# A decoder layer on one core: the output projection in float32r parts, its lower part made on VectorE

## What is computed

```
q = _l2norm((x @ Wq)...); k = _l2norm((x @ Wk)...); v = x @ Wv
alpha = sigmoid(x @ Wg)
S = a_t[..., None] * S + k_t[..., None] * v_t[:, :, None, :]
o_t = einsum('bhkv,bhk->bhv', S, q_t)
return o @ Wo                                   # 8 heads of 128
...
alpha = softmax(X_src @ (X_tgt @ W.T).T); return alpha @ X_tgt
...
h = gelu(x @ Wd[top 2 of 8] + bd) * top_w;  out = h @ Wu + top_w * bu
```

## Time and profile before

| | us |
|---|---|
| three runs | 504.81, 505.24, 506.90 |
| median | 505.24 |
| the profiled execution | 506.75 |
| its span (first to last instruction) | 504.9 |
| PE busy in the span | 469.6 |
| PEld / DVE / ACT / POOL busy | 387.0 / 364.5 / 337.8 / 107.7 |
| Wo matmuls L1232, busy | 60.7 |

### The profile page before, as it was taken

How to read it: one execution, slowest core, us unless ns; L and a number is a source line. 1 busy time by engine, 2 the same in 40 slices (tenths; PEclk the granted TensorE clock), 3 DMA queues, 4 the chain that set the end, 5 groups by cost and what they waited for, 6 DMA issues and landing times.

```text
span 504.9 us, 23866 instructions
## 1 busy us (share of the span) xinstructions
PE 469.6 (93%) x10212; PEld 387.0 (77%) x10212; DVE 364.5 (72%) x1058; ACT 337.8 (67%) x797; POOL 107.7 (21%) x102
## 2 busy tenths in 40 slices
PE   1799999999999999999999999999999999989556
PEld 1588788877888788778888788778888888768334
DVE  5777887655789698774779698774778688863671
ACT  4858777666777857788577867787578858665311
POOL 1022222111221121242121121242022021230130
PEclk9979999999999999999999999999999999998957
DMA  8900000001010010022101010022100010020121
GB/s 325 321 3 5 3 5 3 4 3 44 5 34 15 3 45 3 4 66 66 44 15 34 3 45 4 3 67 65 44 3 5 3 45 3 10 81 0 43 64 61
DMA packets 15256, 20.15 MB, mean 40 GB/s; under 512 B 1200, under 2 KB 12976, under 8 KB 15152
## 3 DMA queue, kind: packets, MB, share of 16 engines
q1 hardware_dynamic: 13872, 14.43, 8.8%
q0 software_dynamic: 1280, 4.20, 2.8%
HBM read 16.53 MB, written 2.10 MB: 37 GB/s over the span
## 4 chain that ended last, share of the span: by engine, by line
PE 49%; DVE 9%; ACT 5%; issue 4%; POOL 1%; DMA 1%; ACTq 0%; DVEq 0%; POOLq 0%
PE ring L1121 13%; PE acc L1232 7%; PE ring L1134 5%; PE lo_bank L1145 5%; PE ring L1213 4%; PE hi_bank L1204 2%; PE ring L1283 2%; PE ring L1220 2%; PE ring L1301 1%; PE ring L1267 1%; PE hi_bank L1176 1%; DVE states L690 1%; PE ring L1293 1%; DVE stats L660 1%; ACT probs L507 1%
## 5 line engine op out<-in xcount | busy, mean ns | idle before, releaser
L466 ACT COPY states<-states 128x512 f32<-128x512 f32 x128 | 80.9, 632 | 46.8 <-DVE states L690 31.2
L379 POOL TENSOR_TENSOR rnorm<-norm_sq,neg_half 128x4 f32<-128x4 f32 x32 | 44.8, 1400 | 267.9 <-DVE norm_sq L753 267.9
L690 DVE TENSOR_TENSOR states<-states,spans 128x512 f32<-128x512 f32 x96 | 66.4, 692 | 10.0 <-PE hi_bank L1176 2.5
L1145 PEld LDWEIGHTS lo_bank<-states 128*32 128x32 f32 x5120 | 51.1, 110 | 23.2 <-issue 19.3
L1232 PE MATMUL acc<-wo_sb,oT_sb 128*128 128x256 f32 x256 | 60.7, 380 | 0.7 <-ACT oT_sb L493 0.7
L1145 PE MATMUL lo_bank<-states 128*32 128x16 f32 (+1 forms) x5120 | 57.9, 188 | 0.0
L741 DVE COPY_PREDICATED blocks<-owned,lo_bank 128x64 f32<-128x64 uint32 (+1 forms) x160 | 41.0, 256 | 22.2 <-PE lo_bank L1145 17.6
L1134 PE MATMUL ring<-wv_sb,xnT 128*128 128x256 f32 x384 | 55.7, 295 | 1.3 <-DVE wv_sb L946 1.3
L1121 PE MATMUL ring<-xnT,wk_sb 128*128 128x512 f32 x192 | 53.7, 416 | 2.0 <-DVE xnT L809 1.6
L1121 PE MATMUL ring<-xnT,wq_sb 128*128 128x512 f32 x192 | 53.4, 413 | 0.0
L1121 PE MATMUL ring<-xnT,wg_sb 128*128 128x512 f32 x192 | 51.8, 406 | 0.4 <-DVE wg_sb L946 0.3
(11 more groups left out here) (157 smaller groups left out, 783.4 us busy)
## 6 DMA issues: line engine op xcount, KB each, us to landing
x_buf<-x_dram SPq DMA_DIRECT2D x4, 512.0 KB, 4.3
ctxT_sb<-ctxT_dram SPq DMA_DIRECT2D x8, 256.0 KB, 3.5
ctx_sb<-ctx_dram SPq DMA_DIRECT2D x4, 512.0 KB, 3.9
out_dram<-x_mid SPq DMA_DIRECT2D x6, 256.0 KB, 2.3
states<-wk_dram SPq DMA_DIRECT2D x1, 1024.0 KB, 5.6
states<-wg_dram SPq DMA_DIRECT2D x1, 1024.0 KB, 7.7
states<-wq_dram SPq DMA_DIRECT2D x1, 1024.0 KB, 9.8
v_sb<-wv_dram SPq DMA_DIRECT2D x1, 1024.0 KB, 11.8
```

The lines of the kernel that those rows point to most:

```text
L379: nc.gpsimd.tensor_tensor(rnorm[:, m % 4, GB:2 * GB], norm_sq[:, GB:2 * GB], neg_half[:, GB:2 * GB], ALU.pow).then_inc(rk_set, 1)
L466: nc.scalar.copy(halves(l, 2 ** (l - 1), False), halves(l - 1, 2 ** (l - 1), False)).then_inc(carry_set, 1)
L690: nc.vector.tensor_tensor(halves(l, w, True), halves(l - 1, w, True), by, ALU.mult).then_inc(decayed, 1)
L1145: last = mm(lo_bank[BLOCK * r:BLOCK * r + BLOCK, to:to + columns], view(states, left + start, [[1, BLOCK]]), view(states, right + start, q ...
```

## The change

- `wo_sb` gets two float32r parts. Wo is loaded by four DMAs (two heads each) into `x_mid` and `rowsT`, which are idle at the start; at the "end" of units 0, 2, 4 and 6 ACT copies the upper part of two heads (128x512) and DVE subtracts the lower (128x512).
- `oT_sb` is float32r with the places HI and LO instead of two alternating buffers. ACT's copy writes HI and now waits until Wo of the unit before has been read (`wo_read_by`); a new DVE instruction `oT_lower(n-2)` reads the same PSUM bank, subtracts HI and writes LO. It stands behind `q_decayed(n+1)` and ahead of tail "late". Wo and the ring's bank wait for it (`oT_lo`).
- Wo of a unit is 12 float32r matmuls of 128x256 instead of 4 float32 ones.
- In the fourth head (h = 3) the eight transposes of the next group's rows move from slot "A" (ahead of `attend`) to slot "B" (behind Wo); ACT's and DVE's reads of them move to the end of the unit.
- `ctx_sb` is now a view of `ctxT_sb`. The plain context is loaded when the transposed one has been used (behind the keys at h = 7), the next transposed one behind the cross attention. So three times the two loads only trade places; the last plain context moves from behind the cross attention of unit 28 to behind the keys of unit 31, and the first is no longer loaded at the start.

```
-        wo_sb = sb("wo_sb", [P, H, D])
+        wo_sb = sb("wo_sb", [P, 2, H, D], F32R)
...
-        ctx_sb = sb("ctx_sb", [P, GB, D])
         ctxT_sb = sb("ctxT_sb", [P, KC, GB, T])
+        ctx_sb = ctxT_sb[:].rearrange("p c b t -> p (c b t)").rearrange("p (b d) -> p b d", b=GB)
...
             if place == "A" and h == 3:
                 found = [("probsT", t, 0)] if t >= 0 else []
-                found += [("xT", i + 1, 0), ("xT", i + 1, 1)] if i + 1 < NG else []
+            if place == "B" and h == 3 and i + 1 < NG:
+                found = [("xT", i + 1, 0), ("xT", i + 1, 1)]
...
-                        "o": (o_set, n + 1), "oT": (oT_set, n + 1)}[kind]
+                        "o": (o_set, n + 1), "oT": (oT_lo, n + 1)}[kind]
...
             for i in range(1, NG):
                 sp.wait_ge(tail_mm, TAIL["keys", i - 1, 1])
-                load_ctxT(i)
+                load_ctx(i - 1)
...
                 sp.wait_ge(tail_mm, TAIL["cross", i - 1, 1])
-                load_ctx(i)
+                load_ctxT(i)
+            sp.wait_ge(tail_mm, TAIL["keys", NG - 1, 1])
+            load_ctx(NG - 1)
...
             def oT_out(n):
                 act.wait_ge(oT_mm, n + 1)
-                nc.scalar.copy(oT_sb[:, n % 2], ring_of(("oT", n))[:]).then_inc(oT_set, 1)
+                if n > 0:
+                    act.wait_ge(*wo_read_by(n - 1))
+                nc.scalar.copy(oT_sb[:, HI], ring_of(("oT", n))[:]).then_inc(oT_set, 1)
...
+            def split_wo(j):
+                act.wait_ge(wo_in, 16 * WO_PAIRS)
+                nc.scalar.copy(wo_sb[:, HI, 2 * j:2 * j + 2].rearrange("p h d -> p (h d)"), stage_o[j]).then_inc(wo_hi, 1)
...
+            def oT_lower(n):
+                dve.wait_ge(oT_set, n + 1)
+                nc.vector.tensor_tensor(oT_sb[:, LO], ring_of(("oT", n))[:], oT_sb[:, HI].bitcast(F32),
+                                        ALU.subtract).then_inc(oT_lo, 1)
...
+                if n >= 2:
+                    oT_lower(n - 2)
                 tail_part(n, "late")
...
             tail_part(U, "late")
+            oT_lower(U - 2)
             o_scaled(U - 1)
+            oT_lower(U - 1)
...
-                    last = mm(accs[z][:, D * m:D * m + D], oT_sb[:, n % 2, T * b:T * b + T], wo_sb[:, h],
-                              start=(h == 0 and m == 0), stop=(h == H - 1 and m == 1))
+                    for part, (a, w) in enumerate(PARTS):
+                        last = mm(accs[z][:, D * m:D * m + D], oT_sb[:, a, T * b:T * b + T], wo_sb[:, w, h],
+                                  start=(h == 0 and m == 0 and part == 0), stop=(h == H - 1 and m == 1 and part == 2))
```

More of the change, by code:

```diff
@@ L101, in decoder_kernel @@
         o_sb = sb("o_sb", [P, GB, P])
-        oT_sb = sb("oT_sb", [P, 2, N])
+        oT_sb = sb("oT_sb", [P, 2, N], F32R)
         x_mid = sb("x_mid", [P, GB, D])
@@ L134, in decoder_kernel @@
         stage_v = v_sb[:].rearrange("p r b h v -> p (r b h v)")
+        WO_PAIRS = H // 2
+        stage_o = tuple(tile[:, 2 * D * k:2 * D * k + 2 * D] for tile in (
+            x_mid[:].rearrange("p b d -> p (b d)"), rowsT[:].rearrange("p c n -> p (c n)")) for k in range(2))
         staged = ((wk_sb, stage_k), (wg_sb, stage_g), (wq_sb, stage_q), (wv_sb, stage_v))
@@ L145, in decoder_kernel @@
         wk_in, wg_in, wq_in, wv_in = (sem(n) for n in ("wk_in", "wg_in", "wq_in", "wv_in"))
+        wo_in = sem("wo_in")
         w_in, c_in, ctx_in, ctxT_in, out_free = (
@@ L158, in decoder_kernel @@
             sem(n) for n in ("decayed", "span_set", "kept", "norm_sq_set", "v_set", "o_set"))
+        oT_lo, wo_hi, wo_split, wo_read = (sem(n) for n in ("oT_lo", "wo_hi", "wo_split", "wo_read"))
         rk_set, rq_set, ln_stat, ln_var, ln_rstd, ln_out = (
@@ L242, in freed_by, with wo_read_by @@
                     "hid": (gelu_set, n + 1), "up": (out_set, pair)}[kind]
+        def wo_read_by(n):
+            i, h = divmod(n, H)
+            return (wo_mm, 2 * i + 2) if h == H - 1 else (wo_read, (H - 1) * i + h + 1)
         def ring_of(name):
@@ L299, in span_at @@
             return 2 * (N // 4 - N // 2 ** l)
-        N_W, N_C = 16 * 4, 16 * 2
+        N_W, N_C = 16 * 3, 16 * 2
         block = stack.enter_context(nc.Block())
@@ L317, in load_ctx @@
             def load_ctx(i):
-                sp.dma_start(ctx_sb[:], ctx[GB * i:GB * i + GB].rearrange("b t d -> t b d")).then_inc(ctx_in, 16)
+                sp.dma_start(ctx_sb, ctx[GB * i:GB * i + GB].rearrange("b t d -> t b d")).then_inc(ctx_in, 16)
             def store(t, z):
@@ L333, in _ @@
                 sp.dma_start(dst[:], src).then_inc(c_in, 16)
-            sp.dma_start(wo_sb[:], wo.rearrange("(h p) n -> p h n", p=P)).then_inc(w_in, 16)
+            for j, heads in enumerate(stage_o):
+                sp.dma_start(heads.rearrange("p (h n) -> p h n", h=2),
+                             wo[2 * P * j:2 * P * j + 2 * P].rearrange("(h p) n -> p h n", p=P)).then_inc(wo_in, 16)
             load_x(1)
@@ L339, in _ @@
             load_ctxT(0)
-            load_ctx(0)
             for i in range(1, NG):
                 sp.wait_ge(tail_mm, TAIL["keys", i - 1, 1])
-                load_ctxT(i)
+                load_ctx(i - 1)
                 if i >= 2:
@@ L544, in tail_part @@
                         gate_exp_out(t)
-                if at == (3, "carry") and i + 1 < NG:
+                if at == (3, "end") and i + 1 < NG:
                     xT_upper(i + 1)
@@ L595, in _ @@
                 tail_part(n, "end")
+                if n < H and n % 2 == 0:
+                    split_wo(n // 2)
             expand_wide(U - 1)
@@ L772, in o_scaled, with split_wo @@
                                         ALU.mult).then_inc(o_set, 1)
+            def oT_lower(n):
+                dve.wait_ge(oT_set, n + 1)
+                nc.vector.tensor_tensor(oT_sb[:, LO], ring_of(("oT", n))[:], oT_sb[:, HI].bitcast(F32),
+                                        ALU.subtract).then_inc(oT_lo, 1)
+            def split_wo(j):
+                dve.wait_ge(wo_hi, j + 1)
+                upper = wo_sb[:, HI, 2 * j:2 * j + 2].bitcast(F32).rearrange("p h d -> p (h d)")
+                nc.vector.tensor_tensor(wo_sb[:, LO, 2 * j:2 * j + 2].rearrange("p h d -> p (h d)"), stage_o[j], upper,
+                                        ALU.subtract).then_inc(wo_split, 1)
             def residual(t):
@@ L925, in tail_part @@
                         ln_normalize(("x", i + 1), x_buf[:, (i + 1) % 2], ("x2T", t, 1) if t >= 0 else ("xT", 0, 1))
-                    if at == (3, "mid"):
+                    if at == (3, "end"):
                         xT_lower(i + 1)
@@ L1224, in output_projection @@
                 i, h = divmod(n, H)
-                pe.wait_ge(oT_set, n + 1)
+                pe.wait_ge(oT_lo, n + 1)
+                if i == 0 and h % 2 == 0:
+                    pe.wait_ge(wo_split, h // 2 + 1)
                 if h == 0:
@@ L1231, in output_projection @@
                     z, m = b // 2, b % 2
-                    last = mm(accs[z][:, D * m:D * m + D], oT_sb[:, n % 2, T * b:T * b + T], wo_sb[:, h],
-                              start=(h == 0 and m == 0), stop=(h == H - 1 and m == 1))
+                    for part, (a, w) in enumerate(PARTS):
+                        last = mm(accs[z][:, D * m:D * m + D], oT_sb[:, a, T * b:T * b + T], wo_sb[:, w, h],
+                                  start=(h == 0 and m == 0 and part == 0), stop=(h == H - 1 and m == 1 and part == 2))
                     if h == H - 1 and m == 1:
                         last.then_inc(wo_mm if i < NG - 1 else half_mm[z], 1)
+                if h < H - 1:
+                    last.then_inc(wo_read, 1)
             def transposed(name):
```

## The result

| | before | after |
|---|---|---|
| median of 19 runs each, us | 505.06 | 509.34 |
| lowest and highest of them | 501.56, 508.18 | 506.98, 512.43 |
| the profiled execution | 506.75 | 508.29 |
| its span | 504.9 | 506.5 |

A forecast was written before the change was run, and what follows sets the result against it. TensorE (93% busy) was taken to bound quiet units, VectorE's gapless chains the row units and the end. Terms -3.2 + 0.9 + 2.1 + 1.1 + 1.3 + 0.3 = +2.5 us gave 507.7 us, range 502.0 to 511.0.

The forecast's parts named there:

- quiet units: Units 4 to 9, 13 to 17, 21 to 25 and 29: VectorE's subtraction is hidden, 17 Wo save 0.19 each, -3.2 us.
- What Wo saves: Every unit's Wo on TensorE: 1.73 us becomes 1.54, saving 0.19 us a unit, 6.1 us for 32.
- The start: Units 0 to 3: splitting Wo delays scaled v by 0.5, Wo of unit 3 waits 0.75, two Wo save 0.38: +0.9 us.
- The row groups: Units 10 to 12, 18 to 20, 26 to 28: VectorE has no gap for the subtraction, +0.7 us each, +2.1 in all.
- The last units: Units 30 and 31: the subtraction delays VectorE's chain to the norm floor and the last expert gathers, +1.1 us.
- The load: Last context load (512 KB) beside the last gathers: between 0 and 1.3 us, taken as +0.3 us.
- The end: Last two Wo: each waits 0.8 us more for the lower part, and the residual comes +1.3 us later.
- rival (c): Around the last two Wo: the 1.2 GHz clock level lasts over both, +5.6 us, 510.8 us; chance 0.12.
- (a): Row units and start: VectorE's chains give way and TensorE's gain is kept, -3.2 us, 502.0 us; chance 0.15.
- (d): Every Wo: float32r beside float32 misses 128 ns, Wo stays at 1.73 or above, +5.7 us, 510.9 us; chance 0.05.
- the late alpha: Sign in the row work: the subtraction makes alpha 0.6 us later; alpha of unit 11 no earlier relative to unit 9.
- the late g behind o_sb: Sign in units 13, 21 and 29: the g projection waits for o_sb, after VectorE's whole 0.6 us in unit 12.

The follow-up runs named there:

- e10_row_work: Kernel before plus one unread 128x512 subtraction on VectorE in each unit from 2 on, Wo left in float32: 508.34 us against 504.72, ratio 1.0071.
- e3_bank: Changed kernel with VectorE's lower part of o moved ahead of the next unit's decays in units 10, 18 and 26: 509.79 us against 504.94, ratio 1.0072.
- e6_ctx: Kernel before with the shared context tile alone, its last load issued beside the last gathers: 504.21 us against 504.87, ratio 0.9998.
- e5_load_lower: Changed kernel with the last context load held until the last gathers landed and lower-part products last in each Wo: 504.39 us, ratio 0.9995.
- e4_gain: Changed kernel without VectorE's lower part of o, the upper part used in its place: 498.38 us against 504.94, ratio 0.9845.

## Why the prediction came out as it did

The time came out on the slower side of the forecast, +4.3 us for +2.5, and the mechanism was in the main the one forecast: TensorE's gain in the quiet units against VectorE's instruction where VectorE has no gap. Three causes were not in it: the bank in unit 26, what the last load costs the gathers where a third transfer lies beside them, and a longer stretch at the low clock. The terms one by one.

**What Wo saves: too small.** 0.19 us was 0.36 in unit 6, and 0.28 to 0.34 a unit in units 4 to 9 and 13 to 17. The step that failed is the choice of the row: I took 187.19 to 188.92, where transposes follow, but in quiet units the levels follow, and up to them Wo takes 1.82. The lead-in from the attention product (0.09) I had not counted. Units 21 to 25 kept only 0.94 for five, because unit 21 became 0.16 longer; e10_row_work shows +0.61 there from the row work alone. Quiet units: forecast -3.2 for 17, measured -4.25 for the same 17 (unit 29 with +0.13).

**The start: right in kind, half in size.** +0.49 in units 1 to 3 for +0.9. Both delays came: TensorE's wait for the scaled v grew from 0.46 to 0.90 us, where I had +0.5, and unit 3 takes 0.7 more than with the lower part last (13.23 against 12.54), where I had 0.75. What was too small is again what the two Wo save: 0.6 to 0.7 in the place of 0.38.

**The row groups: right for two by a ledger that missed a cause, wrong for the third.** +0.79 and +0.81 for +0.7. Units 10 and 11 together +0.29 for +0.1, and unit 12 +0.50 for +0.6, the last by another way than I had it: Wo waits there 0.40 us for the lower part, and the extra work alone leaves the unit as it was (12.94 in e10_row_work). The bank in units 10 and 18 is a wait of 1.2 us that my ledger did not have; e3_bank shows that it cost nothing there, since VectorE's row maximum stood behind it. In unit 26 it counts: +1.54 for +0.7, of which e3_bank takes back 0.84, and e10_row_work shows nothing of it as work. I looked for who waits for VectorE's instruction at Wo and did not follow the bank to its next user, though `freed_by` stood in the diff.

**The last units: right as a sum of work, and a meeting of transfers missed.** +2.85 from v of unit 30 to the second transposes for +1.4. e10_row_work puts the row work at 1.1 us from unit 29 on, as forecast. The load was given 0.3 of a possible 1.3; alone it costs 0.5 in the gathers and nothing that the runs can tell (e6_ctx), and where the packet of q8 is beside it the landing takes 1.9 longer.

**The end: too small.** +1.9 for +1.3. The two waits were forecast (0.51 and 1.40 measured), and from the attention product to the last Wo they cost 1.13 net. The other 0.78 lie ahead of that: the products on the gathered experts, behind 3.7 us of idle TensorE, took 3.75 us where they took 3.50 before (behind 1.46) and 2.02 in e5_load_lower (behind 1.75). The granted clock had fallen to 0.50 there before the change too; rival (c), in which the low level would last over both Wo, did not come (1.00 between 460 and 463 us after the change).

**Rivals.** (a), the gain is kept, did not come about. The Trainium skill's advice ("Perfetto Trace Analysis", Identifying the Most-Contended Engine) is right about TensorE taken alone, since e4_gain is worth 6 us or more; here the faster engine was paid for on one with less occupancy, and e10_row_work shows that its 72% had no room where it counts. (d) fell with 129 ns a product. Of my signs, the wait in units 3 and 11 (in unit 11 it is the first weight load of Wo that waits, 0.24), the late alpha (0.59 later in unit 11, counted from v of unit 9), the late g behind o_sb (0.27 in unit 13) and both last Wo waiting came as said. One sign was ill chosen: "I am wrong if units 8 to 16 take less time than before". They took 1.05 us less (126.26 to 125.21), and by my own terms they should have, 0.7 less 6 x 0.19.

Errors of opposite sign covered each other: the quiet units gave 1 us more, the third group, the last units and the end took 2.9 more, and the start 0.4 less.

## What to carry to other kernels

An instruction that is added to an engine with idle time is paid where that engine's chain has no gap, so cost it unit by unit, and follow not only who waits for its result but also which buffer it holds and who takes that next. Before removing a wait, look at what the waiting work meets next: the edit at the bank took 1.5 us from unit 10, and they came back in unit 11 until VectorE's order was changed there too. Where a result comes in an upper and a lower part, put the products that need only the early part first: the twelve products were the same, and their order alone was worth 2 to 3 us.

## What the runs showed of the hardware that I had not expected

- A float32r group of 128x256 products both starts sooner behind another group (0.81 against 0.90 us) and lets the next one start sooner than the float32 form (129 ns for each of 12, against 1.82 us for the 8 instructions that it replaces, 228 ns each).
- One packet of 16 KB of the instruction queue in the stretch of two other transfers went with 1.4 to 1.7 us more until the rows had landed, though the 16 engines moved 400 GB/s a moment before. That it is the cause is not shown.
- The granted clock in unit 0 and behind the last Wo takes one of two courses, 1.0 us and about 2 us apart, from one kernel's profile to the next. Two profiles of kernels that differ by 4 us can therefore show 1.5. The stretches of quiet units agree better: units 4 to 9 took 75.45 to 75.54 us in five profiles with the old Wo and 73.2 to 73.6 in eight with the new one.
